# Placing one chunk's pattern-score sum ahead of the running sum on VectorE, in the last layer of a two-layer transformer kernel

## What is computed

```
z_sorted = -jnp.sort(-z, axis=-1)
cum = jnp.cumsum(z_sorted, axis=-1)
k = jnp.arange(1, S + 1, dtype=z.dtype)
support = 1.0 + k * z_sorted > cum
tau = (cum_sel - 1.0) / k_sup
return jnp.maximum(z - tau, 0.0)
```

## Time and profile before

| | |
|---|---|
| median of 3 runs | 2151.51 us |
| lowest, highest | 2150.54, 2153.01 us |
| the profiled execution, its own time | 2145.62 us |
| its span, first to last instruction | 2143.9 us |
| mean granted TensorE clock | 0.959 of full |
| TensorE matmul busy | 1973.5 us, 92% |
| VectorE busy | 1549.3 us, 72% |
| ScalarE busy | 1026.7 us, 48% |
| GpSimd busy | 492.4 us, 23% |

### The profile page before, as it was taken

One profiled execution on the slowest core, in us unless ns is written; L12 is line 12 of the kernel. 1 busy time (PEld: TensorE's weight loads), 2 busy tenths in 40 slices (PEclk: granted clock), 3 DMA queues, 4 the chain that ended last, 5 costly groups with the idle time before them and its releaser, 6 DMA issues. The chain is left out here.

```text
span 2143.9 us, 35036 instructions
## 1 busy us (share of the span) xinstructions
PE 1973.5 (92%) x11857; PEld 1190.7 (56%) x11874; DVE 1549.3 (72%) x3492; ACT 1026.7 (48%) x2224; POOL 492.4 (23%) x908
## 2 busy tenths in 40 slices
PE   7869999999999999999579999996878999999998
PEld 3313333333333333332279999995656777777777
DVE  6879888888888888885145333324669998899893
ACT  3406677777777777777444444543331122221112
POOL 4621133322222222222223333335600000000000
PEclk9958999999999999999889999998889999999998
DMA  5572011111111111100332322214510000000005
GB/s 189 186 230 78 29 46 58 56 43 41 41 43 43 42 43 41 43 21 11 92 114 88 110 97 88 89 45 148 167 55 2 18 20 20 20 20 20 3 11 169
DMA packets 119460, 143.69 MB, mean 67 GB/s; under 512 B 12152, under 2 KB 107008, under 8 KB 118912
## 3 DMA queue, kind: packets, MB, share of 16 engines
q1 hardware_dynamic: 89392, 99.48, 14.5%
q0 software_dynamic: 7680, 20.98, 3.1%
q10 hardware_dynamic: 22224, 21.16, 2.9%
HBM read 85.10 MB, written 56.10 MB: 66 GB/s over the span
## 5 line engine op out<-in xcount | busy, mean ns | idle before, releaser
L715 ACT ACTIVATE at_wt<-at_B 128x512 f32<-128x512 f32 (+3 forms) x1280 | 606.9, 538 | 243.0 <-PE at_B L764 237.1
L965 DVE TENSOR_REDUCE at_piece_max<-at_A 128x1 f32<-128x512 f32 x768 | 487.1, 683 | 53.0 <-PE at_A L745 51.1
L782 PE MATMUL at_O<-at_wt,at_v 128*32 128x512 f32 (+3 forms) x2560 | 312.3, 540 | 0.0
L669 POOL TENSOR_SCALAR_AFFINE_SELECT at_wt<-at_wt 128x128 f32<-128x128 f32 x512 | 147.8, 294 | 658.9 <-ACT at_wt L715 650.2
L745 PE MATMUL at_A<-at_k,at_q 96*128 96x512 bf16 (+3 forms) x800 | 275.2, 353 | 8.5 <-DVE at_piece_max L962 2.4
L962 DVE CUSTOM_DVE_ANT_0 at_junk<-at_A,at_hide 128x128 bf16<-128x128 f32 (+3 forms) x512 | 230.3, 487 | 65.9 <-PE at_A L745 62.9
L764 PE MATMUL at_B<-at_q,at_k 99*128 99x512 bf16 (+3 forms) x800 | 272.7, 348 | 2.0 <-ACT at_wt L715 2.0
L1425 PE MATMUL ex_H<-ex_xT,ex_w_in 128*128 128x256 f32 x1920 | 247.4, 285 | 3.2 <-DVE ex_xT L1532 3.2
L1425 PEld LDWEIGHTS ex_H<-ex_xT,ex_w_in 128*128 128x128 f32 x1920 | 236.5, 192 | 3.6 <-DVE ex_w_out L1537 3.6
L1546 DVE TENSOR_TENSOR ex_h<-ex_act_a,ex_H 128x256 f32<-128x256 f32 x160 | 66.8, 417 | 212.4 <-ACT ex_act_a L1474 212.3
L745 PEld LDWEIGHTS at_A<-at_k,at_q 96*128 96x128 bf16 x800 | 77.7, 97 | 214.7 <-DVE at_piece_max L965 108.9
(11 more groups left out here) (262 smaller groups left out, 2633.3 us busy)
## 6 DMA issues: line engine op xcount, KB each, us to landing
buf<-s_down ACTq DMA_DIRECT2D x10, 1024.0 KB, 10.5
ex_x<-buf SPq DMA_DIRECT2D x40, 256.0 KB, 2.7
expert_out<-ex_y ACTq DMA_DIRECT2D x40, 256.0 KB, 2.2
ex_raw_in<-in_W_in SPq DMA_DIRECT2D x8, 1024.0 KB, 4.9
q_parts<-parts SPq DMA_DIRECT2D x16, 384.0 KB, 3.4
s_down<-in_x SPq DMA_DIRECT2D x8, 512.0 KB, 4.8
xn<-xn SPq DMA_DIRECT2D x8, 512.0 KB, 5.6
at_v<-v SPq DMA_DIRECT2D x16, 256.0 KB, 3.4
```

The lines of the kernel that those rows point to most:

```text
L669: pool.affine_select(block_, block_, [[1, P]], ALU.is_ge, 0.0, base=0, channel_multiplier=-1).then_inc(hidden, 1)
L715: act.activation(wt[(HP * p + h) % NE_][:, q0:CH], pB_of(p, h, u)[:, q0:CH], ACT.Exp, scale=D ** -0.5).then_inc(wt_ready, 1)
L782: pe.matmul(pO[j % 2][rows, q0:CH], vs[n % 3][:, kt // TPC, kt % TPC, :], wt[(HP * p + h) % NE_][:, q0:CH], start=kt < 2 and not late, sto ...
L965: ins = dve.tensor_reduce(top, pA[slot % NA][:, 0:w], AX.X, ALU.max)
```

## The change

In an MLP where a part of the next chunk's scores is due (i = 6 to 9) and the running sum (item 30, `SORTS`) is among the items, `keep_scores` is issued right before the running sum, and not behind the items. Item 30 belongs to MLP 7 alone, so what moves is `keep_scores(c + 1, 1)`, once in each chunk c = 0 to 6. In the MLPs 6, 8 and 9 it stays behind the items, and no other engine's stream changes.

```diff
@@ -2276,7 +2276,11 @@
                     hidden(c, i)
                     if c == 0 and i == 0:
                         means()
+                    scored_next = c + 1 < NCH and SCORE <= i < SCORE + TPC
                     for n, item in enumerate(items_of(i)):
+                        if item == SORTS and scored_next:
+                            keep_scores(c + 1, i - SCORE)
+                            scored_next = False
                         if item < SORTS:
                             sort(c, item)
                         else:
@@ -2285,7 +2289,7 @@
                             result(c - 1)
                     if c + 1 < NCH and i == LOW:
                         low(c + 1)
-                    if c + 1 < NCH and SCORE <= i < SCORE + TPC:
+                    if scored_next:
                         keep_scores(c + 1, i - SCORE)
             result(NCH - 1)
```

## The result

The first measurement has the changed kernel at a median of 2139.11 us (6 runs, 2135.28 to 2145.07) and the kernel before at 2150.43 us (6 runs, 2146.95 to 2153.01; the three runs known at the prediction are among them). The ratio is 0.9949, with a 95% interval of 0.9932 to 0.9966: 11 us less, where 5.4 was forecast and 2143.0 was the lower end of the range. Two more measurements of the same kernel, told further down, give 0.9971 and 0.9981. So there are two questions: whether the working held inside the layer, and where the other half of the 11 us came from.

What follows compares the result with a forecast made beforehand. TensorE was taken to set the pace, with VectorE close behind. Six chunks at 0.90 us each, 5.4 us, off the median of 2151.5 gave 2146.1 us, with chunk 0 and the last stage at 0; range 2143.0 to 2150.0 us.

Steps and rivals of the forecast that it cites:

- What moves, and the pause ahead of part 2: Per chunk, take-out and running sum trade places on VectorE; TensorE's pause before score part 2 goes whole, 1.38 us.
- at most 11 us of TensorE's idle time is there to be had: Chunks 1 to 6: TensorE is busy 363.8 of 375 us, which was taken to limit the gain.
- The inherited wait with 0.71 us of cover: The running sum now stands behind a wait for score part 1, ready 0.71 us before VectorE comes: no cost, chunks 1 to 6.
- What is late next: Score part 3 waits for part 2's take-out: 0.48 us of 1.38 comes back, leaving 0.90 us saved per chunk.
- The handover: On VectorE, the independent take-out overlaps the half-step ahead, so everything behind comes about 0.09 us sooner.
- The gain stays, six times: VectorE's waits for TensorE, 1.22 and 2.75 us, let the 0.90 us carry into the next chunk, in chunks 1 to 6.
- Chunk 0: Gives nothing: VectorE idles 1.1 us ahead of the take-out, covered by 1.44 us of idle time, about 0.5 us left.
- A: Rival: the pause goes and none takes its place ahead of part 3; 8.3 us saved, 2143.2 us; 5%.
- B: Rival: VectorE bounds this stretch, so only the handover is left; 0.5 us saved, 2151.0 us; 11%.
- C: Rival: the new pause ahead of part 3 lowers TensorE's clock; each chunk loses 1.50 us, 2160.5 us; 4%.
- How the numbers follow: Closing step setting chances and range: forecast 80%, faster 0.69, same 0.27, slower 0.04; spread from three runs 2.5 us apart.

Runs made afterwards that it cites:

- m1: The change, and in MLP 8 the take-out of part 2 ahead of the maximum, against the kernel before: 2193.82 us, ratio 0.9960.
- m3: The change with the take-outs of parts 0 and 2 also moved ahead of long items, against the kernel before: 2186.14 us, ratio 0.9933.
- p3_front: Take-out of part 1 ahead of the last two sort half-steps in MLP 7, against the kernel before: 2200.49 us, ratio 1.0074.
- n3: The change in chunks 4 to 6 alone, against the kernel before: 2142.42 us, ratio 0.9986.
- n2: The changed kernel again, with more runs on another measurement, against the kernel before: 2140.54 us, ratio 0.9971.
- n4: The change in chunk 0 alone, against the kernel before: 2147.58 us, ratio 0.9995.
- m2: The change, and in MLP 6 the take-out of part 0 ahead of the third sort half-step, against the kernel before: 2188.33 us, ratio 0.9946.
- null kernel: The kernel before, unedited, timed against itself: 2147.38 us, ratio 1.0004.
- p2: Take-outs of parts 0, 1 and 2 each ahead of long items, measured again on the third chip against the kernel before: 2165.27 us, ratio 0.9921.

## Why the prediction was right and where it was wrong

- **What moves, and the pause ahead of part 2**: right. It is gone in all six chunks; m1 shows its worth alone, 1.37 us against the 1.38 read from start to start. The 1.11 us that the row calls idle would have been too little. For the same reason the statement that "at most 11 us of TensorE's idle time is there to be had" is wrong: m3 takes 6 x (62.52 - 60.18) = 14.0 us out of the chunks 1 to 6.
- **The inherited wait with 0.71 us of cover**: right. There is no idle time ahead of the take-out in the chunks 1 to 6, and p3_front, with the cover taken away, has 1.48 us of it and is slower.
- **What is late next**: right in kind and nearly in size. 0.44 us come back ahead of part 3, against 0.48. The forecast that the row itself would read 0.3 to 0.5 us was off: it reads 0.17, by the same difference between idle time and start to start.
- **The handover**: right. The hidden product of MLP 8 starts 6.07 us behind the start of the last half-step (1819.39 to 1825.46), and 6.17 before (1825.32 to 1831.49): 0.10 us against 0.09. By the Trainium skill, page "VectorE: DVE Perf Modes", section "Two Vector instructions with no wait between them", nothing is held here, and the trace agrees.
- **The gain stays, six times**: right; n3 shows it chunk by chunk. 0.96 us against 0.90, 5.8 against 5.4. The idle time that was to be left at the next chunk's first hidden product was put too low, "1.85 us or more": it grew, from 2.75 to 3.19 us. The prediction's own numbers give that, since VectorE comes 1.38 us sooner and TensorE 0.90. The wait of 1.22 us ahead of the hidden product of MLP 9, called one for TensorE, is in its row one for ScalarE's silu; the forecast does not hang on it.
- **Chunk 0**: right, a wait of 1.01 us that is covered. Of the 0.5 us of cover that were to be left, 0.46 are there in n2 and none in the first measurement's trace and in n4, where the clock came back sooner.
- **Rivals**: A's 8.3 us are what m1 shows when the take-out of part 2 is moved too; in the change itself the pause does come. B (VectorE is the bound) is wrong over the chunk, with 3.2 us of wait at its start, but right for the stretch up to part 3, as m2 shows. C does not occur in the change, where the clock stays at 1.00; it is real, as p3_front shows, at 1.7 us for each fall and not the 2.40 us read from chunk 0.

**The step that failed** is in "How the numbers follow", the spread. The range took "the 2.5 us over which the three runs lie" for the spread of a measurement, and 1.2 us of it for the lower end and 1.5 for the upper; for the stages ahead of the layer the sum has no term at all, and it gives no reason for that. The prediction's own numbers spoke against it: the profiled execution of the same kernel, at 2145.62 us, lies 4.9 us below the lowest of the three runs. The runs show what stands in its place. Over 35 runs on one chip the kernel before spreads by 15.6 us (2139.43 to 2154.98) with a standard deviation of 4.4, and the same instructions ahead of the layer end up to 8.5 us apart. A difference between two medians of six such runs has a standard error of some 3 us (an estimate: 4.4 x 1.25 x the square root of 2/6 = 3.2, the factor 1.25 for a median), so the first measurement's 11.3 us is the layer's 5.8 and 1.7 such errors. The three measurements, 0.9949, 0.9971 and 0.9981, lie around the 0.9973 that the layer accounts for. The miss was thus bad luck on top of a range that was too narrow; the mechanism and the size inside the layer were right.

How far chance accounts for the first measurement stays open in part. Its twelve runs by themselves scatter less than the 35 (standard deviations of 3.4 and 2.0 us), and by that scatter the 5 us beyond the layer are about three standard errors (an estimate: 5.2 us between the means beyond the layer's 5.8, against 1.6). What speaks for chance is the null kernel's spread, the unchanged distances in the layer and the two repeats. The profiled pair shows 3.4 us of the rest ahead of the layer, where both kernels are the same; which runs of the first measurement were quick there is not recorded.

## What to carry to other kernels

When an engine in a fixed order holds a short instruction for which another engine waits, put it ahead of the long ones, but not ahead of the moment at which its own input is ready: here 0.7 us of cover was enough, and two half-steps further forward turned a gain of 0.3% into a loss of 0.7%, more than half of it by the clock. Pauses on a chain between two engines have to be costed together and from start to start, because an early take-out is worth nothing while the next one is late, and its full length once that is moved too. Judge a gain of this size by distances inside the trace, which repeat to 0.02 us per chunk (chunk 0 apart, which differs by up to 0.6 us between traces of the same kernel), and give the range of a whole-kernel time from many runs of it, not from three.

## What the runs showed of the hardware

- The same program takes 2147, 2183 or 2201 us on three chips, while each chunk of the last layer takes the same time wherever one kernel was traced on two of them: 61.56 and 61.57 us for the change, 60.18 and 60.18 us for the kernel of m3 and p2. The difference lies ahead of that layer, whose first hidden product comes at 1591 to 1600, 1627 to 1636 and 1644 to 1651 us.
- In p3_front the granted clock fell behind a pause of TensorE of 1.84 to 1.87 us between busy stretches in five chunks, and did not behind one of 1.85 us in a sixth, nor in the chunks 1 to 6 of any other kernel, whose pauses are 1.11 us and shorter. A fall cost 1.7 us.
- A pause of 2.78 us stands ahead of the layer's last down product in all twelve traces. In four (before, m1, m3, p2) the product takes 1.99 us and the granted clock stays at 0.99 to 1.00 over 6 us; in the eight others the product takes 2.40 to 3.65 us at a clock of 0.60 to 0.72. Neither this pause nor the one of 1.85 us settles by its length whether the clock falls.
- VectorE starts an independent instruction 0.08 us before the recorded end of the one ahead, and a dependent one 0.03 us behind it. So each place where two dependent instructions are parted by an independent one is worth about 0.1 us (an estimate; the change shows 0.10 us).
